# First mixture's down products in three 16-bit terms in a four-stage sequence model

## The reference, cut to what matters

```python
logits = x_flat @ gate_w.T
top_v, top_i = jax.lax.top_k(logits, 2)
probs = jax.nn.softmax(top_v)
for e in range(8):
    hidden = silu(x_flat @ wg[e].T) * (x_flat @ wu[e].T)
    out += combine[e][:, None] * (hidden @ wd[e].T)
```

## Time and profile before

| what | us |
|---|---|
| median of 3 runs (lowest, highest) | 1032.54 (1030.79, 1032.74) |
| the profiled execution | 1036.26 |
| its span, first to last instruction | 1034.5 |
| attention, about | 36.6 to 636 |
| units of the first mixture, about | 636.8 to 771 |

### The profile page before, as it was taken

How to read it: one execution, slowest core, us unless ns; L and a number is a source line. 1 busy time by engine, 2 the same in 40 slices (tenths; PEclk the granted TensorE clock), 3 DMA queues, 4 the chain that set the end, 5 groups by cost and what they waited for, 6 DMA issues and landing times. The chain is left out here.

```text
span 1034.5 us, 34747 instructions
## 1 busy us (share of the span) xinstructions
PE 911.2 (88%) x13676; PEld 857.5 (83%) x13676; DVE 732.8 (71%) x1427; ACT 769.0 (74%) x1281; POOL 512.2 (50%) x384
## 2 busy tenths in 40 slices
PE   3789999999999999999999997998989697899940
PEld 2678998998998999888989996997979587899840
DVE  6599989888988988988998993433469877410113
ACT  5689998998998988988989974444565375587840
POOL 5465655655655564654678821322418372053433
PEclk8799999999999999999999997998999798899985
DMA  8400000000000000000001020533201002023221
GB/s 258 131 3 3 23 3 22 3 3 22 3 3 23 3 2 23 2 3 23 8 10 37 14 63 1 180 99 88 57 27 32 11 32 69 14 66 99 65 58 45
DMA packets 43563, 42.13 MB, mean 41 GB/s; under 512 B 5648, under 2 KB 37392, under 8 KB 43408
## 3 DMA queue, kind: packets, MB, share of 16 engines
q1 hardware_dynamic: 39312, 31.51, 10.2%
q0 software_dynamic: 4096, 8.40, 2.8%
HBM read 25.60 MB, written 14.29 MB: 39 GB/s over the span
## 5 line engine op out<-in xcount | busy, mean ns | idle before, releaser
L699 ACT ACTIVATE Pr<-SC,nesc,esc 128x1024 f32<-128x1024 f32 x256 | 310.2, 1212 | 32.9 <-PE SC L511 22.9
L815 DVE TENSOR_TENSOR Pl<-Pr 128x1024 f16<-128x1024 f32 x224 | 293.2, 1326 | 39.7 <-ACT Pr L699 38.1
L510 PE MATMUL SC<-QK 128*128 128x256 f16 x1024 | 238.8, 274 | 1.0 <-ACT QK L681 1.0
L511 PE MATMUL SC<-QK 128*128 128x256 f16 x1024 | 238.9, 274 | 0.0
L536 PE MATMUL OP<-V,Pr 128*128 128x65 f16 x2048 | 214.4, 192 | 6.1 <-DVE Ob L838 5.9
L538 PE MATMUL OP<-V,Pr 128*128 128x64 f16 x2048 | 215.3, 195 | 0.0
L540 PE MATMUL OP<-V,Pl 128*128 128x65 f16 x2048 | 214.1, 191 | 0.0
L536 PEld LDWEIGHTS OP<-V,Pr 128*128 128x128 bf16 x2048 | 191.0, 97 | 12.8 <-issue 8.7
L538 PEld LDWEIGHTS OP<-V,Pr 128*128 128x128 bf16 x2048 | 190.0, 97 | 2.6
L540 PEld LDWEIGHTS OP<-V,Pl 128*128 128x128 f16 x2048 | 190.7, 99 | 0.0
L1066 POOL TENSOR_TENSOR stk<-nrm,stk 128x512 f16<-128x512 f32 x64 | 75.2, 1176 | 139.8 <-DVE stk L797 139.8
(11 more groups left out here) (234 smaller groups left out, 2175.0 us busy)
## 6 DMA issues: line engine op xcount, KB each, us to landing
ys<-yb SPq DMA_DIRECT2D x92, 64.0 KB
w_or_rows<-xs SPq DMA_DIRECT2D x12, 384.0 KB, 4.2
wst<-in_up SPq DMA_DIRECT2D x8, 512.0 KB
xs<-zero SPq DMA_DIRECT2D x2, 1472.0 KB, 13.1
scratch<-in_up SPq DMA_DIRECT2D x4, 576.0 KB
wd<-in_wd SPq DMA_DIRECT2D x4, 576.0 KB
wd<-in_wd SPq DMA_DIRECT2D x4, 512.0 KB
QK<-in_wqkv SPq DMA_DIRECT2D x4, 384.0 KB, 7.4
```

The lines of the kernel that those rows point to most:

```text
L510: eng.matmul(out, QK[:, b, 1, key:key + P], rhs, start=True, stop=False)
L511: mm = eng.matmul(out, QK[:, b, 2, key:key + P], rhs, start=False, stop=True)
L699: eng.activation(Pr[:, n % PB, :, :], SC[s % 2][:, :, :], ACT.Exp, bias=nesc[:, hd:hd + 1], scale=esc[:, hd:hd + 1]).then_inc(s_exps, 1)
L815: eng.tensor_tensor(Pl[:, n % PB, :, :].rearrange("p a b -> p (a b)"), pr, high(pr)[:, 1::2], ALU.subtract).then_inc(s_low_probs, 1)
```

## The change

The down products of the first mixture are made of three 16-bit terms. The fp32 tensors `wd0` become pairs `wd0h`, `wd0l`. In the second to fifth pair of heads (`i` from 1 to 4) SP brings one 512 KB part of the down weights into `wst` ahead of the up weights, ACT copies its halves in slots 5 and 9, and DVE subtracts in slots 7 and 11. The four loads at the start go. In every unit DVE makes `hid_low` behind `hid`; the high part of `hid` is read in place as the upper 16 bits. Every down product waits for `hid_low` of its tile.

```diff
+DOWN_FIRST = 1
+DOWN_HIGH_AT = (5, 9)
+DOWN_LOW_AT = (7, 11)
...
-        for c in range(NC):
-            eng.dma_start(t["wd0"][c][:, :], io["wd0"][:, E * P * c:E * P * c + E * P]).then_inc(self.s_down, 16)
...
-        eng.wait_ge(self.s_down, 16 * NC)
...
             def load(i):
 
                 wait(eng, s_up_low, 2 * i)
+                if splits_down(i):
+                    c = i - DOWN_FIRST
+                    eng.dma_start(wst[:, :], io["wd0"][:, E * P * c:E * P * c + E * P]).then_inc(s_down_loaded, 16)
+                    eng.wait_ge(s_down_low, 2 * c + 2)
...
+            def high_down(c, m):
+                at = slice(FF * m, FF * m + FF)
+                eng.wait_ge(s_down_loaded, 16 * c + 16)
+                eng.activation(t["wd0h"][c][:, at], wst[:, at], ACT.Copy).then_inc(s_down_high, 1)
...
+            def low_down(c, m):
+                at = slice(FF * m, FF * m + FF)
+                eng.wait_ge(s_down_high, 2 * c + m + 1)
+                eng.tensor_tensor(t["wd0l"][c][:, at], wst[:, at], t["wd0h"][c][:, at],
+                                  ALU.subtract).then_inc(s_down_low, 1)
...
                 if l == 0:
-                    if u + LAG2 >= 2 * TILES:
-                        eng.wait_ge(s_hidden, u + 1)
+                    eng.wait_ge(s_hidden_low, u + 1)
...
                 for c in range(NC):
-                    mm = eng.matmul(DB[:, 0:D], hid[:, u % HR, P * c:P * c + P], wd[l][c][:, at], start=c == 0,
-                                    stop=c == NC - 1)
+                    cs = slice(P * c, P * c + P)
+                    if l == 0:
+                        hi, lo, wh, wl = (high(hid[:, u % HR, cs])[:, 1::2], hid_low[:, u % HR, cs],
+                                          t["wd0h"][c][:, at], t["wd0l"][c][:, at])
+                        eng.matmul(DB[:, 0:D], hi, wh, start=c == 0, stop=False)
+                        eng.matmul(DB[:, 0:D], hi, wl, start=False, stop=False)
+                        mm = eng.matmul(DB[:, 0:D], lo, wh, start=False, stop=c == NC - 1)
+                    else:
+                        mm = eng.matmul(DB[:, 0:D], hid[:, u % HR, cs], wd1[c][:, at], start=c == 0, stop=c == NC - 1)
...
                 eng.tensor_tensor(hid[:, u % HR, :], act[:, u % 2, :], UB[u % 2][:, :], ALU.mult).then_inc(s_hidden, 1)
+                eng.wait_ge(s_hidden, u + 1)
+                h = hid[:, u % HR, :]
+                eng.tensor_tensor(hid_low[:, u % HR, :], h, high(h)[:, 1::2], ALU.subtract).then_inc(s_hidden_low, 1)
```

More of the change, by code:

```diff
@@ L81, with splits_down @@
 UP_LOW_AT = (20, 28)
+DOWN_FIRST = 1
+DOWN_HIGH_AT = (5, 9)
+DOWN_LOW_AT = (7, 11)
+def splits_down(i):
+    return DOWN_FIRST <= i < DOWN_FIRST + NC
 def low_count(n, pool):
@@ L179, in __init__ @@
         self.int_iota = sb("int_iota", [P, TILES], mybir.dt.int32)
-        self.s_loaded, self.s_down, self.s_zero, self.s_cleared, self.s_made, self.s_sum, self.s_exp = (
-            sem(n) for n in ("c_loaded", "c_down", "c_zero", "c_cleared", "c_made", "c_sum", "c_exp"))
+        self.s_loaded, self.s_zero, self.s_cleared, self.s_made, self.s_sum, self.s_exp = (
+            sem(n) for n in ("c_loaded", "c_zero", "c_cleared", "c_made", "c_sum", "c_exp"))
     def sync(self, eng):
@@ L333, in attention @@
         s_up_loaded = sem("s_up_loaded")
+        s_down_loaded, s_down_high, s_down_low = sem("s_down_loaded"), sem("s_down_high"), sem("s_down_low")
         s_up_high = sem("s_up_high")
@@ L730, in slot @@
                     prepare(h + 1, (s // SLOTS + 1) % 2, sh)
+                if s in DOWN_HIGH_AT and splits_down(i):
+                    high_down(i - DOWN_FIRST, DOWN_HIGH_AT.index(s))
                 if s in UP_HIGH_AT and not ended(i):
@@ L992, in slot @@
                         read_out(i - 1, s + 2 * SLOTS - 4)
+                if s in DOWN_LOW_AT and splits_down(i):
+                    low_down(i - DOWN_FIRST, DOWN_LOW_AT.index(s))
                 if s in UP_LOW_AT and not ended(i):
@@ L1222, in mixtures @@
         up = ((t["w0h"], t["w0l"]), (w1h, w1l))
-        wd = (t["wd0"], wd1)
         split = sb("split", [P, B, TB, 2 * D], F16)
@@ L1228, in mixtures @@
         act = sb("act", [P, 2, FF], F32)
+        hid_low = sb("hid_low", [P, HR, FF], F16)
         hid = sb("hid", [P, HR, FF], F32)
@@ L1272, in mixtures @@
         s_split_high, s_split_low = sem("split_high"), sem("split_low")
+        s_hidden_low = sem("hidden_low")
         s_scattered = [sem(f"scattered{i}") for i in range(4)]
@@ L2106, in program @@
             "w0l": [sb(f"w0l{c}", [P, E * P], F16) for c in range(2 * NC)],
-            "wd0": [sb(f"wd0{c}", [P, E * P], F32) for c in range(NC)],
+            "wd0h": [sb(f"wd0h{c}", [P, E * P], F16) for c in range(NC)],
+            "wd0l": [sb(f"wd0l{c}", [P, E * P], F16) for c in range(NC)],
             "gate": sb("gate", [P, E], F32),
```

## The result

The changed kernel takes **1064.35 us** (median of 4 runs, 1063.33 to 1065.68) against 1031.66 for the kernel before in the same comparison (4 runs, 1030.21 to 1032.74): ratio 1.0324, 95% interval 1.031 to 1.0338, so 32.7 us slower. The forecast was 1055 in a range of 1044 to 1064: right side, too small by 9.35 us, and the result lies just outside the range.

The account below looks back on a forecast made before the run. The prediction took PE's queue of register instructions as the bound of the changed units. Its terms, 17.8 + 0.5 - 0.5 + 0.6 + 4.4 = +22.8 us on the median 1032.54, gave 1055, range 1044 to 1064.

Parts of the forecast that it names:

- the rival with three: Down products: three register instructions for each `c`, 28 a unit, +35.5 us, with the rest 1073; chance 0.07.
- The array did not stay the bound: Rival for the units: the array stays the bound, a unit takes 2.11 us, total 1028; chance 0.10.
- fp32's four passes against three terms: Down products by the skill's rule: 0.22 us gained a unit, about 1032; same rival as the array staying the bound.
- The sign: Whole kernel: slower 0.88, faster 0.10, same 0.02.
- the queue as the bound: Units: PE's queue sets the pace at 24 register instructions of 0.12 us; 1055, range 1044 to 1064; chance 0.80.
- the attention, +4.4 taken: Splitting weights beside pairs two to five: 1.1 us a pair, four pairs, +4.4, between 0 and 6.
- at most 1.4 a pair: Attention: upper end of the splitting's cost for each pair, in us, less the slack; at least nothing.
- attention free: Rival: the splitting in the attention costs nothing, total 1051, inside the range; no chance of its own.
- the unit, +0.48 taken: Units: four more register instructions, 2.9 us against 2.45; 37 of 46 units pay 0.48, +17.8.
- my bound of 0.6 a unit: Units: upper bound of the growth, some 3.05 us a unit against 2.45; lower bound +0.3.
- its ends: Stage's first four units +0.5 us, last four +0.6; one low-clock unit after the wait gains about 0.5.
- The correction of 3.7 us: Whole kernel: the profiled 1036.26 us was 3.7 above the median 1032.54, so 1059 became 1055.

Follow-up runs that it names:

- the third trace: The kernel before, no edit, profiled again: median 1031.61 us, a trace of 1032.91 us.
- the first trace: The kernel before, no edit, as profiled for the prediction: an execution of 1036.26 us.
- the second trace of the changed kernel: The changed kernel run again, no edit: 1064.1 us against 1031.39 for the kernel before, ratio 1.0318.

## Why the prediction was wrong in size

*Right, step by step.* The bound of the units is PE's queue and not the array: taking four register instructions out takes 0.46 us out of a unit with the same matmuls. There are eight at the down products, two for each `c`; the rival with three falls by the counts. The array did not stay the bound, and fp32's four passes against three terms brought nothing. `hid_low` is 46 times 0.69 us, and PE never waits for it within the stage. No wait for one of the new loads appears. The granted clock from 671 to 706 is 1.00. The sign stands, and the queue as the bound, which had 0.80, came true.

*Wrong: the attention, +4.4 taken, 10.2 us measured in the pairs.* The mechanism I named (DVE has no slack from slot 5 to 14, each subtraction makes Ob late) is there and about its size: the fourth pair, which kept its meeting harmless, is 1.2 us longer, 0.6 at each of the two subtractions, where I took 1.1. What failed is the sentence that this is "at most 1.4 a pair" and the bound of 6. I followed the lag only up to the waits for Ob. But a lag of 1 us on DVE also changes which of two engines has to wait for the other, and the three other pairs paid **1.7 us more** each for a Pl of DVE behind POOL's. The rows to see it by were in the trace of before: POOL's Pl of 2.35 us at 141.84, overlapping DVE's, against 1.89 alone. The rival "attention free" falls too.

*Wrong: the unit, +0.48 taken, 0.56 measured.* The four register instructions are 0.46 of it. The other 0.12 is the semaphore instruction: the change gives the down product a second wait, and I had counted what stands behind a wait and when it is met, but not that a second wait is an instruction of its own on the queue that sets the pace. Joined to another wait it gave back 3.45 us, or 0.09 for each of 37 units. The kernel before avoided just this, by waiting for `hid` only in the last units. Over the 37 units that I had let pay, the growth against the third trace is 19.5 us (0.53 each), where I had written 17.8; my bound of 0.6 a unit held. With its ends the stage grew by 20.6, where my terms make 18.4.

*The sum.* 5.8 us missing in the attention and 2.2 in the stage are 8.0 of the 9.35. The rest lies between traces and medians: the two traces differ by 30.8 us (1063.71 against 1032.91), the medians by 32.7, and no trace shows that difference. The correction of 3.7 us from the profiled execution to the median was right: the pauses that lengthen two traces of before are missing in the third. Held against the first trace alone the stage would have grown by 17.0, and the forecast of it would look good by luck.

*What stays open.* What the pauses of PE's queue in some comparisons are. They do not belong to one chip: the same chip gave the kernel before 1031.39 us in one comparison and 1036.16 in another. And why DVE wins one meeting and loses three with starts only 0.02 to 0.03 us apart; in the second trace of the changed kernel it was another pair that it won.

## What to carry to other kernels

On a queue that sets the pace, count instructions and not matmuls: here a run-time address and a second wait cost about 0.12 us each, whatever the matmuls behind them do, so a cheaper arithmetic with one more address a step was slower. Join a new wait to one that already stands there and implies it. Where two engines' operations of over 1 us already overlap in a trace, find out which one is made longer before delaying either: a lag on one of them can be paid twice, when the order turns.

## What the runs showed of the hardware

Two elementwise operations of DVE and POOL, alone 1.22 and 1.89 us, take 2.95 on DVE or 2.99 on POOL when they start together; the loser ends 1.1 us (DVE) or 1.8 us (POOL) after the winner, about its own length. A semaphore instruction on PE's queue, shown as 51 ns, takes 0.12 us of the pace (3.01 to 2.89 us a unit) though its condition had long been met. A matmul of 256 moving columns with two planes (step of the plane 1024 elements) needs one register instruction for its address (48 at line 1508 in 12 units), like one of 128. And the median of one unchanged kernel was 1031.4, 1031.7, 1031.9, 1035.5, 1036.2 and 1037.5 us in six comparisons.
